# The last half piece of the down product: 128 rows instead of 64 for its low weights

## What is computed

```python
g = jax.lax.ragged_dot(xs, w_gate, group_sizes)
u = jax.lax.ragged_dot(xs, w_up, group_sizes)
d = jax.lax.ragged_dot(jax.nn.silu(g) * u, w_down, group_sizes)
...
shared = jax.nn.silu(x @ sw_gate) * (x @ sw_up) @ sw_down
return (expert_out + shared).reshape(B, S, H)
```

## Time and profile before

| what | us |
|---|---|
| median of the three runs | 6870.29 |
| the three runs | 6862.52, 6870.29, 6919.63 |
| span of the profiled execution, which is also its time | 6862.4 |
| TensorE matmuls busy in it | 6482.2 (94%) |
| GpSimd busy in it | 3159.8 (46%) |

### The profile page before, as it was taken

The page is one execution under the profiler, slowest core; times in us unless marked ns, Lnnn a source line. Parts: engine busy times, 40 slices in busy tenths (PEclk is TensorE's granted clock), DMA queues, the critical chain, the costliest instruction groups (busy, mean ns, idle before and its releaser), DMA issues.

```text
span 6862.4 us, 89812 instructions
## 1 busy us (share of the span) xinstructions
PE 6482.2 (94%) x32230; PEld 3068.5 (45%) x32231; DVE 1716.0 (25%) x2906; ACT 1036.0 (15%) x1564; POOL 3159.8 (46%) x2065
## 2 busy tenths in 40 slices
PE   3777699999999999999999999999999999999998
PEld 1333344444444444444444444444444444444444
DVE  7998730011111111111111111111111111115555
ACT  3444301111111111111111111111111111110000
POOL 2444643464444564444654456444564466443222
PEclk9888799999999999999999999999999999999999
DMA  2333469985555565555655556555565566548787
GB/s 88 135 141 128 155 217 294 338 281 148 142 142 144 151 165 152 140 142 146 167 155 147 140 149 167 158 142 142 153 165 152 139 165 171 142 142 263 255 258 228
DMA packets 1146762, 1175.27 MB, mean 171 GB/s; under 512 B 867296, under 2 KB 867296, under 8 KB 1146720
## 3 DMA queue, kind: packets, MB, share of 16 engines
q10 hardware_dynamic: 902352, 477.20, 29.3%
q1 hardware_dynamic: 184464, 487.80, 21.5%
q0 software_dynamic: 59904, 209.75, 8.5%
HBM read 647.63 MB, written 327.16 MB: 142 GB/s over the span
## 4 chain that ended last, share of the span: by engine, by line
PE 85%; issue 6%; POOL 4%; DMA 2%; DVE 2%; ACT 0%; DVEq 0%; POOLq 0%; ACTq 0%; SPq 0%
PE ps_gu L635 56%; PE ps_d L635 25%; DMA hT<-hid_hl 2%; PE ps_d L776 2%; PE ps_d L774 2%; POOL wts L485 1%; POOL wts L499 1%; POOL wts L489 1%; POOL wts L479 0%; POOL wts L503 0%; DVE wts L1362 0%; DMA wts<-in_ctx 0%; DVE max_rows L1084 0%; POOL wts L476 0%; POOL stage L477 0%
## 5 line engine op out<-in xcount | busy, mean ns | idle before, releaser
L635 PE MATMUL ps_gu<-wts,xT 128*128 128x512 f16 (+1 forms) x19584 | 3930.8, 362 | 9.2 <-DVEq L1402 4.0
L635 PEld LDWEIGHTS ps_gu<-wts,xT 128*128 128x128 f16 x19584 | 1895.0, 98 | 2040.9 <-issue 122.6
L635 PE MATMUL ps_d<-wts,hT 128*128 128x512 f16 x8160 | 1814.9, 380 | 30.2 <-DMA hT<-hid_hl 30.2
L476 POOL TENSOR_SCALAR wts<-stage 128x1408 f16<-128x1408 f32 (+1 forms) x476 | 585.9, 1231 | 2259.9 <-PE ps_d L776 2241.4
L1314 DVE SCALAR_TENSOR_TENSOR hid<-ps_gu,sil 128x704 f32<-128x704 f32 x272 | 242.5, 892 | 4579.1 <-ACT sil L970 4579.1
L479 POOL TENSOR_TENSOR wts<-stage,wts 128x1408 f16<-128x1408 f32 (+1 forms) x476 | 1231.6, 2587 | 39.7
L635 PEld LDWEIGHTS ps_d<-wts,hT 128*128 128x128 f16 x8160 | 800.0, 98 | 987.5 <-DMA hT<-hid_hl 25.7
L970 ACT ACTIVATE sil<-ps_gu 128x704 f32<-128x704 f32 x272 | 205.9, 757 | 2855.9 <-PE ps_gu L635 2855.9
L477 POOL TENSOR_SCALAR stage<-stage 128x1408 f32<-128x1408 f32 (+1 forms) x476 | 624.1, 1311 | 0.0
L992 ACT ACTIVATE dout<-ps_d 128x1024 f32<-128x1024 f32 x240 | 245.8, 1024 | 2168.4 <-DMA xT<-xin 1951.6
L635 PE MATMUL ps_d<-wts,xin 128*128 128x512 f16 x1536 | 391.5, 418 | 75.6 <-DVE xin L1104 54.8
(11 more groups left out here) (163 smaller groups left out, 2103.4 us busy)
## 6 DMA issues: line engine op xcount, KB each, us to landing
rows_d<-dout ACTq DMA_DIRECT2D x240, 512.0 KB, 3.4
xin<-rows_x ACTq DMA_DIRECT2D x211, 512.0 KB, 3.3
stage<-in_L_ffn_w_down SPq DMA_DIRECT2D x384, 256.0 KB, 3.2
stage<-in_L_ffn_w_gate SPq DMA_DIRECT2D x256, 352.0 KB, 3.2
stage<-in_L_ffn_w_up SPq DMA_DIRECT2D x256, 352.0 KB, 3.7
wts<-in_x SPq DMA_DIRECT2D x64, 512.0 KB, 3.7
rows_x<-wts SPq DMA_DIRECT2D x64, 512.0 KB, 2.9
wts<-rows_x SPq DMA_DIRECT2D x64, 512.0 KB, 7.0
```

What stands on the lines that cost most here:

```text
L476: g.tensor_scalar(high, raw, WSCALE, 1.0, ALU.mult, ALU.mult).then_inc(conv_step, 1)
L635: ins = nc.tensor.matmul(dst[c], left, right[c], start=(first and a == 0), stop=(last and a == 2))
```

## The change

The two matmuls with the low weights use all 128 rows of `hT` and of `wts`, as the two with the high weights do. They thereby add the product of the low hidden part with the low weight part, which was left out before. The argument `rows` of the helper falls away, and the two loops become one.

```diff
-                def weights(half, k, rows=P):
+                def weights(half, k):
                     at = GU + k * H
-                    return [wts[0:rows, buf, half, at + c * 512:at + (c + 1) * 512] for c in range(2)]
+                    return [wts[:, buf, half, at + c * 512:at + (c + 1) * 512] for c in range(2)]
...
-                for c in range(2):
-                    nc.tensor.matmul(outs[c], hT[:, u, KM - 1, :], weights(0, KM - 1)[c], start=False, stop=False)
-                for c in range(2):
-                    ins = nc.tensor.matmul(outs[c], hT[0:M_LAST, u, KM - 1, :], weights(1, KM - 1, M_LAST)[c],
-                                           start=False, stop=True)
+                for half in range(2):
+                    for c in range(2):
+                        ins = nc.tensor.matmul(outs[c], hT[:, u, KM - 1, :], weights(half, KM - 1)[c], start=False,
+                                               stop=half == 1)
                 ins.then_inc(down_done, 1)
```

## The result

The changed kernel takes 6809.31 us (median of four runs, 6796.65 to 6828.4), against 6872.11 us for the kernel before (four runs, 6862.52 to 6919.63). The ratio is 0.992, with a 95% interval from 0.989 to 0.995. In a second comparison, the fourth experiment, it was 0.990 (0.983 to 0.997). So the change saves some 0.8%, as forecast.

A forecast was written before the change was run, and what follows sets the result against it. TensorE's own matmuls bound the kernel; 263 × 0.199 = 52.3 us plus 0.1 us makes 52.4 us saved. That gives 6810.0 us from the profile, 6817.9 from the median; predicted between them 6814 us, range 6798 to 6850.

The forecast's parts named there:

- What bounds the kernel: A tile costs TensorE's time for its own matmuls, 21.807 us; whatever is cut there comes out of the time.
- One sign: In the changed profile, ScalarE's and GpSimd's waits for PE should shrink by no more than 0.2 us a tile.
- The two late steps: In each down product, the switches into 64 rows and out again cost about 0.1 us each; both would go.
- The step out of the 64 rows: From a down product's last matmul to the next gate_up: the whole 0.10 us was taken to go.
- branch and waits are its price: Rival: only the switch into 64 rows goes, 0.10 x 264 = 26 us, giving 6836 to 6844; chance 0.08.
- I take 0.199 us, between the two ways: Gain per tile from both switches, between 0.197 us from the four matmuls and 0.20 us from the whole tile.
- Its other term: In the 8 tiles where PE waited for hidden values the gain is lost, leaving 263 full gains of 271.
- A load of another height is not taken ahead: At the 64-row matmuls, a load with another row count waits until the engine finishes: 0.42 us idle a tile.
- The rule against the change: The two new 128-row loads would stand in the open, 2 × 0.098 us, no gain: 6862 us; no chance of its own.
- Late transposes: Rival: from 1077 to 1480 us, more late transposes at 10.4 us each use up much of the gain; chance 0.08.
- the sum that starts from the profile: The profiled execution's span of 6862.4 us less the gain of 52.4 us gives 6810.0 us.
- From 4 to 70 us in hand: Other engines' margins ahead of PE: VectorE 4.1 and ScalarE 10.5 us a tile, GpSimd 70 us a weight change.

The follow-up runs named there:

- the fourth experiment: The changed kernel run again, unedited, in a second comparison with the kernel before: 6814.84 us (median of four), ratio 0.990.
- the first experiment: Kernel before with the half piece's four matmuls in the order 128, 64, 128, 64 rows, four switches for two: 6918.82 us against 6867.3.
- the pair inside the product: Kernel before with the two 64-row matmuls moved behind the down product's second whole piece, the 128-row ones at its end: 6882.79 us, one run.

## Why the prediction was right, and where it was off

**What bounds the kernel: right.** Cutting 0.209 us a tile from PE gave 63 us less by the medians (6872.11 − 6809.31), and adding 0.210, in the first experiment, gave 51.5 us more. The arithmetic is 56.6 and 56.8; what the medians have above and below it lies within the scatter of the runs. No engine took PE's place. One sign did not come as named: the wait of ScalarE for PE was to shrink by no more than 0.2 us a tile and shrank by 0.37. In part it moved to the wait for the transposed tile, which the prediction had not looked at; the forecast did not suffer.

**The two late steps: right, both.** That the starts, not the durations, had to be read is confirmed; the mean durations of the groups of the half piece are 377 to 387 ns in every kernel here. The step out of the 64 rows was the uncertain one. The rival that branch and waits are its price is refuted by the changed profile (0.87 us for all four steps) and by the pair inside the product.

**Their size: 5% too small.** The term "I take 0.199 us, between the two ways" measured 0.209. The gap is 10 ns in the second matmul behind the step out of 64 rows, which falls into gate_up: its 14.27 us, which I took as free of the switch, held this, and are 14.26 in the changed kernel. The sum would have been 263 × 0.209 = 55.0 us in place of 52.3. Its other term, that 8 late tiles lose their gain, could not be measured: such a loss shows as a longer wait, and the waits differ from run to run by far more than 8 × 0.2 us.

**"A load of another height is not taken ahead": too wide.** 96 rows after 128 are taken ahead. It is a change between the modes of 128 rows and of 64 or 32 that stops the loads; for 64 rows the two readings cannot be told apart, so the forecast did not suffer.

**The rule against the change.** The page "TensorE: Matmul & The Clock Gate" of the Trainium skill (Part 3, The mechanism) has loads overlap only with matmuls of another row group. The measurement decides against it: the 128-row loads of the half piece start 0.118 us after the end of the load ahead, one step before their own matmuls and thus beside a matmul on the same rows, and the steps are ordinary ones. By the rule, as the prediction works it out, the time would have been 6862 us.

**Late transposes.** They did not grow clearly with the faster tiles. In the stretch from 1077 to 1480 us, where the prediction feared them, the tiles took 31 us beyond their period in place of 29. But they decide which run one looks at: the two profiles compared alone show 35.7 us of a gain of 56.6. So it is partly luck that 6809.31 came within 5 us of the forecast of 6814 and within 1 us of the sum that starts from the profile (6810.0; from the median it was 6817.9): the gain was put 4 us too low, and the runs of the changed kernel alone lie 32 us apart.

**A margin I overstated.** "From 4 to 70 us in hand" is made of means, for GpSimd over 32 changes of weights. At the first routed expert there may be no such margin: two of ten profiles have PE waiting there, both with the slower tile. The faster tile brings PE to that point some 32 × 0.209 = 6.7 us earlier, so in a run with a late scatter that much of the gain is given back. No run shows it for the changed kernel.

## What to carry to other kernels

On a matmul stream, compare the steps between starts with the ordinary step: modelled durations and "idle before" of the matmuls hide a lost 0.1 us, and the idle time before the loads shows it. A pair of matmuls of 64 or 32 rows among full ones cost two changes of mode here, 0.21 us, and a single one as much, and filling it up to 128 rows (or to 96) with data that does no harm was free. When one profile is compared with one other, take out the waits that come by chance first, and read the gain from the period of undisturbed tiles.

## What was not expected of the hardware

- 96 rows ran without a switch (21.602 us a tile), while 64 and 32 rows cost the same 0.209 us.
- Two 64-row matmuls on the two halves of the rows, with different column halves as output, ran side by side, which was one of three outcomes that I allowed for: 0.39 us for both, 0.387 us being the length of one.
- The switch slows the step after it, too: the second matmul behind it takes about 10 ns more than the ordinary 216 ns.
